# Moving the output projections one step later and the transposes of the next x two steps later in an attention loop

## The reference

```python
x = _ln(src) * (1.0 + scale) + shift
q = (x @ Wq + bq).reshape(B, S, N_HEAD, HEAD_DIM).transpose(0, 2, 1, 3)
...
scores = jnp.einsum('bhqd,bhkd->bhqk', q / math.sqrt(HEAD_DIM), k)
scores = scores + attention_bias
scores = jnp.where(src_mask, -jnp.inf, scores.astype(jnp.float32))
probs = jax.nn.softmax(scores, axis=-1).astype(v.dtype)
ctx = jnp.einsum('bhqk,bhkd->bhqd', probs, v)
ctx = ctx.transpose(0, 2, 1, 3).reshape(B, S, D)
x = x + (ctx @ Wo + bo)
h = _ln(x) * g2 + beta2
ff = _gelu2(h @ W1 + b1) @ W2 + b2
return x + ff
```

## Time and profile before

| what | value |
|---|---|
| median of 3 runs | 994.39 us (993.97 to 995.47) |
| profiled execution, its own time | 993.79 us |
| span of the profiled execution | 992.0 us |
| PE busy | 928.4 us, 94% |
| DVE busy | 749.0 us, 76% |
| POOL busy | 701.3 us, 71% |
| ACT busy | 690.1 us, 70% |
| moved by DMA | 229.96 MB |

### The profile page before, as it was taken

The page is one execution under the profiler, slowest core; times in us unless marked ns, Lnnn a source line. Parts: engine busy times, 40 slices in busy tenths (PEclk is TensorE's granted clock), DMA queues, the critical chain, the costliest instruction groups (busy, mean ns, idle before and its releaser), DMA issues. The chain is left out here.

```text
span 992.0 us, 19948 instructions
## 1 busy us (share of the span) xinstructions
PE 928.4 (94%) x5758; PEld 615.4 (62%) x5838; DVE 749.0 (76%) x2000; ACT 690.1 (70%) x1126; POOL 701.3 (71%) x542
## 2 busy tenths in 40 slices
PE   5879989999998999999999899979999999999996
PEld 5646556655655655665565566545577777777574
DVE  7888788878879787887986878788444765677565
ACT  3577888898788798879878888888644444545333
POOL 1788788788878869878886977877554545567465
PEclk9999999999999999999999999999999999999998
DMA  8988988996996899699689779965111110111101
GB/s 289 326 311 299 381 300 284 340 376 219 333 387 253 294 380 346 234 339 383 238 294 390 282 267 343 368 250 207 64 64 43 43 43 22 43 65 43 43 22 64
DMA packets 127533, 229.96 MB, mean 232 GB/s; under 512 B 6512, under 2 KB 53872, under 8 KB 123632
## 3 DMA queue, kind: packets, MB, share of 16 engines
q1 hardware_dynamic: 127472, 229.26, 63.8%
HBM read 187.30 MB, written 41.94 MB: 231 GB/s over the span
## 5 line engine op out<-in xcount | busy, mean ns | idle before, releaser
L938 ACT ACTIVATE prob<-prob,nmax 128x512 f32<-128x512 f32 x512 | 356.6, 728 | 56.7 <-DVE nmax L760 53.9
L760 DVE CUSTOM_DVE_ANT_0 prob<-s_bank,big 128x512 f32<-128x512 f32 x512 | 338.7, 685 | 63.4 <-POOL big L1102 30.3
L1102 POOL TENSOR_TENSOR big<-big,mterm_early 128x2048 f32<-128x2048 f32 (+2 forms) x88 | 305.7, 3488 | 73.9 <-DMA big<-in_fside_Bx16xSxS 57.6
L591 PEld LDWEIGHTS t_bank<-ident,prob 128*128 128x128 f32 x2048 | 239.8, 141 | 167.5 <-issue 51.7
L591 PE MATMUL t_bank<-ident,prob 128*128 128x128 f32 x2048 | 318.6, 278 | 18.3 <-ACT prob L938 7.1
L945 ACT COPY pt<-t_bank 128x512 f32<-128x512 f32 x312 | 181.0, 583 | 55.4 <-PE t_bank L591 54.2
L769 DVE COPY pt<-t_bank 128x512 f32<-128x512 f32 x200 | 137.3, 687 | 40.0 <-PE t_bank L591 39.8
L579 PE MATMUL s_bank<-stack_k,stack_q 128*128 128x512 bf16 x432 | 165.0, 382 | 2.2 <-DVE nmax L760 1.6
L605 PE MATMUL o_bank<-pt,val 128*32 128x512 f32 x1024 | 122.9, 598 | 3.7 <-issue 1.0
L2201 POOL TENSOR_TENSOR gl<-big,gh 128x512 fp32r<-128x512 f32 x64 | 83.0, 1305 | 49.6 <-DVE gh L1743 49.6
L2052 ACT ACTIVATE big<-bank,late 128x512 f32<-128x512 f32 x62 | 42.6, 689 | 72.6 <-PE bank L1450 69.1
(11 more groups left out here) (247 smaller groups left out, 1454.8 us busy)
## 6 DMA issues: line engine op xcount, KB each, us to landing
big<-in_fside_Bx16xSxS SPq DMA_DIRECT2D x128, 1024.0 KB, 8.0
pieces_dram<-pieces SPq DMA_DIRECT2D x64, 384.0 KB, 7.2
stack_q<-pieces_dram SPq DMA_DIRECT2D x15, 1024.0 KB, 7.8
stack_k<-pieces_dram SPq DMA_DIRECT2D x15, 1024.0 KB, 9.7
pieces_dram<-pieces SPq DMA_DIRECT2D x32, 256.0 KB, 7.4
xin<-in_x SPq DMA_DIRECT2D x8, 512.0 KB, 8.6
x_dram<-x SPq DMA_DIRECT2D x8, 512.0 KB, 2.6
x1r<-x_dram SPq DMA_DIRECT2D x8, 512.0 KB, 4.3
```

Source lines behind the costliest of these rows:

```text
L591: last = pe.transpose(t_bank[n % 2][:, c * P:(c + 1) * P], prob[:, n % NT, c * P:(c + 1) * P], ident[:])
L760: dve.tensor_tensor_reduce(out=prob[:, n % NT, :], in0=s_bank[n % 3][:, :], in1=bias[:, h % NB, t, :], scale=-1.0, scalar=3e38, op0=ALU.ad ...
L938: act.activation(tile, tile, ACT.Exp, bias=nmax[:, n % NT:n % NT + 1], scale=-1.0).then_inc(exped.sem, 1)
L1102: pool.tensor_tensor(bias[:, h % NB, tiles], bias[:, h % NB, tiles], mterm[:, tiles], ALU.add).then_inc(masked.sem, 1)
```

## The change

Two lists are edited. The output projections start in steps 11 and 13 in place of 10 and 12; the transposes of the next x are done in steps 16 and 17 in place of 14 and 15. The order of the jobs, and so the bank of each, stays. DVE's residual adds move from steps 12 and 14 to 13 and 15, its writes of xt from 15 and 16 to 17 and 18. The steps of "T" in the last iteration are not changed.

```diff
-TAIL = [("O", 3, 6, 1), ("C", 0, 7, 1), ("C", 1, 9, 1), ("W", 0, 10, 1), ("W", 1, 12, 1)]
-AHEAD = [("XT", 0, 14, 0), ("XT", 1, 15, 0), ("Q", 0, 21, 0), ("K", 0, 23, 0), ("Q", 1, 28, 0), ("K", 1, 29, 0)]
+TAIL = [("O", 3, 6, 1), ("C", 0, 7, 1), ("C", 1, 9, 1), ("W", 0, 11, 1), ("W", 1, 13, 1)]
+AHEAD = [("XT", 0, 16, 0), ("XT", 1, 17, 0), ("Q", 0, 21, 0), ("K", 0, 23, 0), ("Q", 1, 28, 0), ("K", 1, 29, 0)]
```

## The result

| | before | after |
|---|---|---|
| median of the runs compared | 994.18 us (990.27 to 996.08) | 1030.84 us (1025.23 to 1033.31) |
| profiled execution, its own time | 993.79 us | 1027.1 us |
| span | 992.0 us | 1025.3 us |

The ratio is 1.0361, with a 95% interval from 1.0341 to 1.0381: the change makes the kernel some 36 us slower. I had predicted 988.2, in a range from 984.5 to 993.0, and given "slower" a chance of 0.09.

The account below looks back on a forecast made before the run. PE, busy about 80 of 84 us, bounds most of an iteration. Leads of 3.30, 2.75 and 0.30 make 6.35, 0.80 passed on: 5.1; plus 1.1 in the last, 6.2 us gained: 988.2 us, range 984.5 to 993.0.

Parts of the forecast that it names:

- SP's queue: DMA issue: head 8's bias load goes out earlier, at a DMA share of 0.38, and collides with nothing.
- Does DVE keep up?: DVE: x ready near 225.1 instead of 226.48; low parts run from 233.3 to 235.3, just in time for Q0.
- From turn(14) to the weighted sum: PE, steps 14 to 17: stretch shrinks from 4.47 to 3.77 us; the sum starts 1.08 us earlier.
- XT0 no longer waits: PE: first transposes of the next x find it ready, removing a 1.30 us wait in iteration 2.
- Rival 3: Q0: late xt write delays the low parts, each of seven iterations loses 1.3 us; about 1001 us, chance 0.05.
- Rival 4: PE: clock falls in all six iterations, 10 us lost against 6.2 gained; 998 us, chance 0.04.
- Iteration 6: Loop iteration 6: loses what set off its slow-clock stretch, a lead of 0.66 + 2.09 = 2.75 us.
- Iteration 0: Loop iteration 0, without projections: only transposes leave the stretch behind exp(14); gain 0 to 0.6 us, taken as 0.3.
- Last iteration: Final iteration: waits before the first projection and turn(16) shrink; gain 1.1 us, bounds 0.62 and 1.49.
- Rival 1: Next iteration's head 1 bias: DMA takes leads back, only the last iteration gains; 993.3 us, chance 0.12.
- Rival 2: PE: new stall for exp(14) slows the clock in one to three iterations, 1.67 us each; 990 to 993, chance 0.14.

Follow-up runs that it names:

- experiment 7: Kernel after, plus three POOL waits: late mask terms and iteration 0's head 5 mask for normalised x, head 7's mask for low parts: 984.7 us, ratio 0.9916.
- experiment 9: Kernel after, plus one wait: POOL's mask addition for head 7, and so head 8, waits for the low parts of x: 988.54 us, ratio 0.9952.
- W alone: Kernel before, with only the output projections moved, to steps 11 and 13: 996.53 us, ratio 1.0016.
- XT alone: Kernel before, with only the transposes of the next x moved, to steps 16 and 17: 1023.94 us, ratio 1.0238.
- experiment 2: Kernel after, with POOL's mask addition for head 8 made as four 128 x 512 instructions in place of one 128 x 2048: 1001.38 us, ratio 1.007.

## Why the prediction was wrong, step by step

**SP's queue** is where it failed first. The step saw that head 8's load goes out earlier and priced that by the share of DMA bandwidth: "it collides with nothing". Bandwidth was the wrong thing to ask. The transfer was what kept POOL quiet while DVE made the low parts: POOL's 2.31 us of waiting for it was their cover, as much as W had been the cover of exp(14). An earlier load took it away, and the step should have asked what POOL does when the data is there.

**Does DVE keep up?** used the low parts' 2.02 us of the earlier trace rows as if it were the work's own duration. It was 1.42 held by head 7's mask and 0.68 by itself, in a place where POOL then stopped. The part that starts just behind POOL's 4.19 us addition takes 4.54. The start was near: 14.68 after the first W, where I said 233.3 - 218.66 = 14.64. The end was at 21.36 in place of 235.3 - 218.66 = 16.64.

The same step also had x ready near 225.1 and three passes of the normalisation in front of the late mask. In the kernel after head 5's mask ran until 227.09 and held the first pass, which ended 0.15 behind it, and the late mask terms started at 227.18 beside the other three. The four passes together take 2.53 us in iteration 2 and 3.35 in iteration 1. They end 7.1 to 7.9 us after the first W, against 7.8 to 8.3 before and the 225.1 - 218.66 = 6.4 that I counted on: a gain of 0.2 to 0.8 in place of 1.4. The price was in the earlier trace rows (407 alone, 793 beside POOL); I wrongly took the overlap away. With the waits of experiment 7 they take 1.38 in iteration 2 and end 5.9 to 6.5 after the first W.

**From turn(14) to the weighted sum.** I predicted 9.57 us from the first W; it was 9.58 in iteration 2 and 9.92 to 10.40 in the others. The hit in iteration 2 is luck: there head 5's mask holds the first pass for least. The missing 0.35 to 0.8 goes with the passes of x: with the low parts alone freed (experiment 9) it is still 9.72 to 10.36, with all waits (experiment 7) 9.45 in each iteration. PE's wait for exp(14) was 1.47 in each, predicted 1.25, and "XT0 no longer waits" held everywhere. So the PE side of the estimate was right to a few tenths, as far as PE's own work goes.

**Rival 3**, "slower: the x chain is late for Q0", had the right place and the right sign, and it was to decide from low parts ending 0.9 late; they ended 21.36 - 16.64 = 4.7 late. But it had a late xt write as its cause, and that wasn't late: the second one ended 13.54 after the first W, where I had 232.1 - 218.66 = 13.44. And it had a price of 1.3 per iteration. The measured one is 6.0, because the hold is 4 us in one piece and a slow stretch of the clock follows it. Hence 1001 for 1031, and a chance of 0.05.

**Rival 4, the clock.** Behind the stall that I watched, the 1.47 for exp(14), it didn't fall in any iteration. It fell with the one that I hadn't, the 4.42 at Q0.

**Iteration 6** lost its old slow stretch as predicted, and got the new one of iterations 2 to 5. **Iteration 0**, priced at a gain of 0.3, contributed up to 2.85 of loss. The fourth pass of its normalisation is held by head 5's mask. PE's clock falls behind the wait for exp(14), as before, but is low for 10.2 us from 53.94 in place of 3.4. The step list is the same up to that point, so the change did not place this collision: W alone has it too, the other profiles haven't, and the pass and the mask miss each other by tenths of a microsecond. Its timeline, and the stretch of the slow clock, kernel after:

```profile
52.24 5.23 DVE L799 TENSOR_SCALAR xin<-xin,mv,rstd 128x256 f32<-128x256 f32 x4
...
53.25 4.06 POOL L1102 TENSOR_TENSOR big<-big,mterm_early 128x2048 f32<-128x2048 f32 x1 [2.09 <-DMA big<-in_fside_Bx16xSxS]
```

```profile
53.90:64.20 10.30, 7.87 (x34) 3.29 (x31) 7.41 (x11) 4.89 (x9) 9.90 (x6) 0.50 1.02 368
```

**Last iteration:** gain 0.48, predicted 1.1, bounds 0.62 to 1.49. **Rival 1** (the DMA takes the lead back) can't be judged in the kernel after, where there was no lead; in kernel 7 iterations of 82.76 to 83.29 against 83.51 to 84.21 show that it doesn't hold. **Rival 2** needed the slow clock behind the new stall in one to three iterations; it was there in none.

With POOL out of the way change and waits together bring more than the 6.2 us predicted for the change, and kernel 7's span of 982.9 against 992.0 says where. Iterations 1 to 6 take 630.53 - 132.43 = 498.10 for 504.73, which is 6.6 where I had 4.8 (5.1 less iteration 0's 0.3). Most of the rest is iteration 0, which ends 2.5 earlier. Its low parts take 2.03 there for 5.25 before, while its normalisation ran clear of the mask in both and its clock is low for longer (6.8 us for 3.4). How much of the 2.5 the waits brought is open: over the twelve profiles the first W of iteration 1 comes anywhere from 132.3 to 140.6, and with XT alone, without a wait, at 133.8.

## What to carry to other kernels

When a change makes a load leave earlier, ask what its consumer will run over once the data is there. An engine's idle gap can be the cover of another engine's work, and no list of waits shows that. When the same instruction has a maximum many times its minimum (4544 to 673 ns here), look for the instruction of the other engine that it overlaps, and order the two by a semaphore: three waits on POOL took the kernel after from 1030.84 to 984.7 us.

## What the runs showed of the hardware that I had not expected

**A DVE instruction between SBUF tiles waits for the whole POOL instruction that is running.** The 128 x 512 subtraction with two SBUF inputs takes 0.68 us alone and 4.54 under POOL's 4.19 us addition, and 1.64 when that addition is cut in four. Wherever in the addition it starts, from 0.06 to 3.3 us behind POOL's start, it ends 0.54 or 0.55 behind POOL's end, in every held part of the eleven profiled kernels with whole additions; one that starts ahead of POOL's takes 0.68 (iteration 1 of the kernel after). An operation with one SBUF input can be held too: the fourth normalise pass of iteration 0 took 4.25 us under a POOL addition of 4.06, and the passes held by such an addition in iterations 1 to 6 end 0.15 behind its end. The same pass with its input in PSUM, in the last iteration, takes 0.53 in the middle of such an addition: it isn't held. Beside POOL's short conversions (2.71 for four) a pass takes 0.775 in place of 0.41. The Trainium skill, GPSIMD Engine Reference, "Key points", says that GpSimd shares its SBUF interfaces with VectorE, with contention for DVE instructions in a 2-port perf mode or with two SBUF inputs. The trace agrees on the subtraction and puts a number to it. Whether the single-input pass is in such a mode no run here shows.

**The clock falls with a stall of 4.4 us and is low for 3.4 or 6.8.** It went to 0.50 (1.2 of 2.4 GHz) in each of iterations 2 to 6, for 6.8, 6.8, 3.4, 3.4 and 6.8 us. The fall came between 2.2 us ahead of Q0's start, inside the wait, and 0.55 behind it, and it didn't come when PE had 34 matmuls to do in the wait. With Q0's wait of 2.91 (XT alone) the clock fell in all five as well; with 1.52 (experiment 2) or the 1.47 for exp(14) in none; with 1.49 in iteration 6 of the kernel before it did. I had counted on a stall costing its own length; this one cost about half as much again: 2.2 us in iteration 2 (25.80 - 23.57) on a wait of 4.42.
